# The causal mask of a decoder's self-attention, added by products of 64x64 quarters of TensorE's array

## What is computed

```python
q = jnp.einsum('ntc,hdc->nhtd', x_q, w_q)
k = jnp.einsum('ntc,hdc->nhtd', x_q, w_k)
v = jnp.einsum('ntc,hdc->nhtd', x_q, w_v)
a = jnp.einsum('nhtd,nhsd->nhts', q, k) / math.sqrt(q.shape[3])
causal_forbidden = jnp.arange(t)[:, None] < jnp.arange(t)[None, :]
a = jnp.where(causal_forbidden[None, None], -jnp.inf, a)
a = jax.nn.softmax(a, axis=3)
y = jnp.einsum('nhts,nhsd->nthd', a, v).reshape(a.shape[0], t, -1)
return y @ w_o
```

## Time and profile before

| | |
|---|---|
| median of 3 runs | 300.07 us (299.88 to 300.49) |
| profiled execution | 300.5 us |
| its span, first to last instruction | 298.3 us |
| TensorE busy (products) | 281.7 us, 94% |
| TensorE weight loads | 178.6 us, 60% |
| VectorE, ScalarE, GpSimd busy | 214.7, 192.6, 146.9 us |
| mean granted TensorE clock | 0.999 |

### The profile page before, as it was taken

One profiled execution on the slowest core, in us unless ns is written; L12 is line 12 of the kernel. 1 busy time (PEld: TensorE's weight loads), 2 busy tenths in 40 slices (PEclk: granted clock), 3 DMA queues, 4 the chain that ended last, 5 costly groups with the idle time before them and its releaser, 6 DMA issues.

```text
span 298.3 us, 6631 instructions
## 1 busy us (share of the span) xinstructions
PE 281.7 (94%) x2446; PEld 178.6 (60%) x2446; DVE 214.7 (72%) x481; ACT 192.6 (65%) x481; POOL 146.9 (49%) x267
## 2 busy tenths in 40 slices
PE   0899899999999999999999999999999998999995
PEld 0567666666666669666666677444454553347674
DVE  3668778878776660886876747987888869457854
ACT  2487587777877780777777830777777767735343
POOL 3606867885577792388555500078309174000241
PEclk9999999999999999999999999999999999999999
DMA  7930000000000000000000000000000000000001
GB/s 277 285 138 3 0 3 1 2 2 0 3 2 3 0 2 2 0 3 2 1 2 2 2 2 0 2 0 0 2 0 1 3 0 3 0 0 2 0 26 46
DMA packets 4835, 6.17 MB, mean 21 GB/s; under 512 B 834, under 2 KB 3650, under 8 KB 4676
## 3 DMA queue, kind: packets, MB, share of 16 engines
q1 hardware_dynamic: 4228, 5.29, 5.1%
q10 hardware_dynamic: 576, 0.47, 0.5%
HBM read 5.23 MB, written 0.52 MB: 19 GB/s over the span
## 4 chain that ended last, share of the span: by engine, by line
PE 80%; DVE 7%; POOL 5%; ACT 4%; issue 1%; DMA 1%; ACTq 0%; DVEq 0%
PE bank L748 70%; PE bank L819 7%; DVE qk L1472 3%; POOL pr L338 2%; POOL cw_sb L415 1%; POOL qk L421 1%; DMA x_sb<-in_x 1%; DVE nmax L1427 1%; PE bank L971 1%; ACT pr L564 1%; POOL pT L338 1%; DVE stats L1344 1%; PE bank L873 1%; PE bank L1056 1%; ACT pT L564 1%
## 5 line engine op out<-in xcount | busy, mean ns | idle before, releaser
L663 ACT ACTIVATE pT<-bank 128x512 f32<-128x512 f32 (+1 forms) x80 | 44.6, 601 | 25.6 <-PE bank L748 25.2
L564 ACT ACTIVATE pr<-bank,nmax 128x256 f32<-128x256 f32 (+2 forms) x96 | 44.4, 480 | 22.8 <-DVE nmax L1427 22.5
L1472 DVE TENSOR_REDUCE qk<-bank 128x4 fp32r<-128x616 f32 x64 | 49.1, 795 | 13.6 <-PE bank L748 13.5
L338 POOL TENSOR_SCALAR pr<-pr,pinv 128x256 f32<-128x256 f32 (+2 forms) x96 | 45.8, 495 | 23.6 <-DVE pinv L1435 23.4
L748 PE MATMUL bank<-qs 64*128 64x256 f32 (+3 forms) x256 | 49.5, 470 | 0.3 <-ACT qs L543 0.3
L1427 DVE TENSOR_REDUCE nmax<-bank 128x2 f32<-128x512 f32 (+2 forms) x48 | 31.7, 688 | 11.4 <-PE bank L748 11.2
L748 PE MATMUL bank<-pT,v_sb 128*64 128x128 f32 (+2 forms) x320 | 38.6, 385 | 0.0
L338 POOL TENSOR_SCALAR pT<-pT,pinv 128x512 f32<-128x512 f32 x32 | 22.1, 703 | 22.9 <-DVE pinv L1435 22.9
L1443 DVE COPY pT<-bank 128x512 f32<-128x512 f32 (+1 forms) x32 | 30.3, 948 | 1.4 <-PE bank L819 1.4
L748 PEld LDWEIGHTS bank<-pT,v_sb 128*64 128x64 f32 x320 | 21.0, 136 | 13.9 <-issue 10.5
L748 PE MATMUL bank<-km,qk 64*128 64x308 f32 x128 | 27.7, 367 | 1.2 <-DVE qk L1472 1.1
(11 more groups left out here) (192 smaller groups left out, 573.8 us busy)
## 6 DMA issues: line engine op xcount, KB each, us to landing
pT<-in_wqk SPq DMA_DIRECT2D x1, 1024.0 KB, 6.0
cw_sb<-in_cw SPq DMA_DIRECT2D x1, 768.0 KB, 8.9
x_sb<-in_x SPq DMA_DIRECT2D x2, 256.0 KB, 5.3
pT<-in_wv SPq DMA_DIRECT2D x1, 512.0 KB, 6.8
wo_sb<-in_wo SPq DMA_DIRECT2D x1, 512.0 KB, 7.1
out<-x_sb SPq DMA_DIRECT2D x6, 64.0 KB, 1.6
onT<-in_consts ACTq DMA_DIRECT2D x1, 256.0 KB, 6.3
pT<-in_xwk SPq DMA_DIRECT2D x1, 256.0 KB, 7.2
```

The lines of the kernel that those rows point to most:

```text
L338: nc.gpsimd.tensor_scalar(d, d, pinv[:, t, a:a + 1], 1.0, ALU.mult, ALU.mult).then_inc(norm_done, 1)
L564: nc.scalar.activation(prob[r][:, a, at:at + w], bank[:, SP[k % 2] + a, at:at + w], ACT.Exp, bias=nmax[:, t, a:a + 1], accum_out=psum[:, t ...
L663: nc.scalar.activation(px[rows, i, :], bank[rows, (ST0, ST1)[i % 2], :], ACT.Exp, scale=SD ** -0.5).then_inc(xexp_done, 1)
L1472: nc.vector.tensor_reduce(m, s_in, AX.X, ALU.max, negate=True).then_inc(round_done, 1)
```

## The change

The four products of a burst keep their number and order, but each becomes a quarter of the array. `half` 0 has stationary columns 0 to 63 and writes partitions 0 to 63; `half` 1 has columns 64 to 127 and writes partitions 64 to 127. A product is thus 64 rows by 64 columns at one of the four corners. `half` 0 still streams the 128 mask columns; `half` 1 streams the upper 64 alone, for queries 64 to 127 mask no key of the diagonal block below 64.

```diff
--- before.py
+++ after.py
@@ -787,8 +787,9 @@
                     for half in range(2):
                         for a in range(2):
                             own = slice(64 * a, 64 * a + 64)
-                            last = mm(bank[:, SP[k % 2] + a, at - P:at], sel_b[own, half, :], mask_b[own, half, :], False,
-                                      half == 1, skip_group_check=True)
+                            rows = slice(64 * half, 64 * half + 64)
+                            last = mm(bank[rows, SP[k % 2] + a, at - P + 64 * half:at], sel_b[own, half, rows],
+                                      mask_b[own, half, 64 * half:P], False, half == 1, skip_group_check=True)
                 last.then_inc(s_ps, 1)
 
             def turn(n, r):
```

## The result

The changed kernel takes 308.70 us (median of 5 runs, 307.77 to 309.30), the kernel before 300.07 (299.56 to 300.49). The ratio is 1.0276, with a 95% interval of 1.0260 to 1.0292: 8.6 us slower.

A forecast was written before the change was run, and what follows sets the result against it. TensorE was taken as the attention's bound. Form-change gaps and bare loads, less shorter bursts, gave 0.905 us a step, 13.6 over 15 steps, plus 0.6 for step 0, less 0.6 absorbed: 300.07 + 13.6 = 313.7 us; range 310.5 to 319.5.

The forecast's parts named there:

- TensorE bounds the attention, a step's growth is the kernel's: In 36 to 165 us TensorE idles 0.60 us of 129, so one microsecond of TensorE is one of the kernel.
- Going in 0.10, way out 0.095: At each mask burst, changing the array's form costs a gap of 0.10 us before and 0.095 us after.
- Rivals 2 and 3: At the bursts: only one side pays, about 307, chance 0.08; no drain at all, 297.2, chance 0.08.
- the sign: Whole kernel slower, chance 0.90; a burst loses once its gaps and bare loads together pass 0.045 us.
- Products 0.065 us, corners together: In a burst all four quarters run together: 0.055 us plus 0.01 stagger, in place of 0.11.
- rival 1: In each burst the halves run in turn, 0.08 us more x 64 = 5.1 us: 318.8; chance 0.12.
- Load of a quarter 0.05 us: At each burst, a quarter's uncovered weight load takes 0.05 us, from the f32 row with as many columns.
- the lower bound that I named, 0.01: At each burst, a quarter's load as fast as today's, 0.01 us, would take 2.6 us off: 311.1.
- 0.10 for the load of tile 0's scores: Behind round 2's first burst, the scores' uncovered load adds 0.10 us; that burst grows by 0.30.
- No other engine can hide more: In the attention, VectorE, ScalarE and GpSimd follow TensorE, each under 80% busy, so they absorb no further loss.
- 0.6 us absorbed: Other waits, TensorE's idle in 36 to 165 us and part of that in 27 to 36, take 0.6 off 14.2.
- Clock: Rival: emptier stretches lower TensorE's clock for a tenth of the stage, 13 us more, 327; with anything unnamed, chance 0.04.

## Why the prediction was right in sign and wrong in size

- *TensorE bounds the attention, a step's growth is the kernel's*: right as a sum (0.59 us for each of 15 steps less 0.6 of idle is 8.2 us, as measured from the first mask product to the last; 8.6 in time), wrong in "TensorE's own work and nothing else". A constant period doesn't tell work from a wait that returns in every step.
- *Going in 0.10, way out 0.095*: right, in each burst of all kernels with quarters. Rivals 2 and 3 fall with it; the sign too hung on this. Quarters where the way out is paid anyway, and scores as quarters, show that it is the change of form.
- *Products 0.065 us, corners together*: right (0.055 and a stagger of 0.01); rival 1 falls by the run with full-width quarters and by the scores as quarters.
- *Load of a quarter 0.05 us*: a term mis-sized, 0.024 measured. The f32 row with as many columns was the wrong neighbour; for bf16 the load is half as long. Going in, burst and way out together were 0.31 us by the forecast and are 0.27: 0.026 of the 0.04 is the load, the rest rounding and stagger. x 64 = 2.6 us of the 5.0. The load lies between the lower bound that I named, 0.01, and what I took. That the 2.6 us equal what I gave for the lower bound is chance: the load alone makes 1.7 of them. The range should have been built from this term and the next two together.
- *0.10 for the load of tile 0's scores*: half of it was paid before. From those scores to their burst it is 0.28 us before (106.08 to 106.36) and 0.42 after, 0.14 more and not 0.20; one part of the 0.11-us load was always longer than the burst that covered it. 0.05 x 16 = 0.8 us.
- *"No other engine can hide more"; 0.6 us absorbed*: the step that failed outright. With the wait in the sum, the forecast would have been 1.5 us nearer. The 0.6 of idle was absorbed, and beside it 0.095 us a step of a wait for ScalarE, 1.5 us. I had read the waits and the busy shares, which can't show it, and not the distance of starts behind the transposes, which does: 0.54 in place of 0.50.
- 2.6 + 0.8 + 1.5 = 4.9 of the 5.0 us between forecast and result. No term alone explains the miss: had the hidden wait been the only error, the time would have been 312.2 us, inside the range.
- *Clock*: it held, as forecast.

The Trainium skill's page "TensorEngine Tiling (Array Packing)" (Key Properties) has the engine drain when the tiling mode changes. The runs here agree for 64x128 against 64x64 too, with 0.10 us each time.

## What to carry to other kernels

Before you split a small product over more corners of TensorE's array, count the changes of form towards its neighbours, at 0.10 us and a bare weight load each in this kernel, and only then the columns saved. No run here made quarters pay: with the scores as quarters too, and four added changes a step, the kernel was still 2.0 us slower than before. On an engine that looks fully busy, measure the distances between starts of like groups; where sixteen transposes take 0.54 us in one place and 0.50 in another, there is a wait that will swallow part of any loss and part of any gain. And shortening a product below the load behind it brought nothing here.

## What the runs showed of the hardware that I had not expected

- A change of form costs the same 0.095 to 0.10 us whichever of rows and columns changes, at 64 array rows too. A change from f32 to bf16 in one form costs no gap.
- The bare load behind it, in this kernel: 0.11 us for 128 columns of f32, 0.05 for 64 of f32, 0.05 for transposes' 128, 0.024 for 64 of bf16.
- Four 64x64 corners stream together at full rate, f32 (eight products of 512 columns in 0.91 us, four of 64x128 in 0.92) and bf16 (four starts within 0.01 us).
